# Half of the message sums of a graph network as one-pass products of a rounded part and its rest

## The chip, the cores and the metric

The kernel runs on one core of a Trainium2 chip. A core has a matrix engine (TensorE, PE in the profile; PEld are its weight loads), a vector engine (VectorE, DVE), a scalar engine (ScalarE, ACT), GpSimd (POOL) and a queue for transfers (SyncE, SP). All run at the same time and wait for each other on counters. The metric is device time of the whole program in microseconds (us); lower is better. Before the change three runs gave a median of 3258.17 us (3254.01 to 3269.35).

## The reference

The program is two layers of a graph network with attention, a gated recurrence and experts over 2048 nodes of 512 numbers. The change touches one step, the messages of the second layer:

```
# xn: (2048, 512), edge_attr: (32768, 64), W_e: (64, 512)
msg = jax.nn.relu(x[src] + edge_attr @ W_e + b_e)
aggr = jax.ops.segment_sum(msg, dst, num_segments=x.shape[0])
h = (1.0 + eps) * x + aggr
```

Each of 32768 edges takes the row of its source node, adds its own 64 attributes times a matrix, clips at zero, and is added to the row of its destination node. The inputs `xn_rows` already contain `b_e`. Everything is float32.

## The kernel before

An earlier stage has sorted the edges by destination into buckets of 128 destination rows, padded to whole tiles of 128 edges. A table `sorted_edge` holds for each edge its 64 attributes, the place of its destination within the bucket and its source. Tiles are worked on in pairs: `EG` = 144 pairs, and a pair is of one bucket. For pair `n` these steps run:

- gather (POOL, L2672): two indirect transfers fetch the 2 x 128 source rows into `src`, which has room for four pairs.
- pack (ACT, L2710): once in eight pairs, the attributes are laid side by side in `att`, 64 columns of either tile.
- turn (PE, L2687), eT (ACT, L2716): the 128x128 attributes are transposed into a PSUM bank and copied out as `eT`.
- edge (PE, L2692): two products with `we`, one with the upper and one with the lower 64 rows, into two PSUM banks (banks 2 to 7 serve three pairs in turn).
- raw (DVE, L2738): two additions of 128x512, bank plus `src` into `msg` (three pairs).
- relu (ACT, L2719): clips `msg` in place, 128x1024 in one instruction.
- hot (DVE, L2730): for two pairs at once, the one-hot matrix `hot` of the destinations.
- sum (PE, L2700): two products `hot` by `msg`, accumulated in bank 0 or 1. It sums the messages per destination. Each float32 product is carried out as two instructions.
- add (DVE, L2749): adds the bank to the rows of the bucket in `acc`, at an offset read from a table.

The order on each engine is written by a list: every step of pair `n` has a due time `n + at` (gather -3.6, turn -2.3, eT -2.2, edge -1.75, raw -1.4, relu -0.85, sum 0, add 0.6, hot -2.2), the list is sorted by it, and each engine takes its own steps in that order. An engine's queue is strictly in order: a step that waits holds back all behind it. The waits are those for data (`raw` for the gather and for the edge products, `relu` for `raw`, ...) and those for free buffers (gather `n` for raw `n - 4`, raw `n` for sum `n - 3`, sum `n` for add `n - 2`).

Of the kernel before, what the change touches and what calls it, by code (L numbers as in the profile page):

```python
# [5 lines left out]
F32 = mybir.dt.float32  # L6
I32 = mybir.dt.int32
F32H = mybir.dt.float32r
BF16 = mybir.dt.bfloat16
ALU = mybir.AluOpType  # L10
AF = mybir.ActivationFunctionType
AX = mybir.AxisListType

P = 128
N, D = 2048, 512
# [144 lines left out]
def program(nc, I, const_at, out):  # L160
    PE, ACT, DVE, POOL, SP = nc.tensor, nc.scalar, nc.vector, nc.gpsimd, nc.sync
    everyone = (PE, ACT, DVE, POOL, SP)
    ctx = ExitStack()
    with ctx:
        sig = Signals(nc, ctx)
        pairs = [ctx.enter_context(nc.psum_tensor(f"bank{2 * i}", [P, 2, 512], F32)) for i in range(4)]
        bank = [pairs[i // 2][:, i % 2, :] for i in range(8)]
# [65 lines left out]
        sb = tensors(perf, "perf")  # L233
# [17 lines left out]
        sb = tensors(early, "sort")  # L251
# [23 lines left out]
        hot, run = (va2[:, i * NK * EC:(i + 1) * NK * EC].rearrange("p (b c) -> p b c", b=NK) for i in range(2))  # L275
        src, dst = ends[:, 0, :], ends[:, 1, :]
# [346 lines left out]
        sb = tensors(late, "mix")  # L623
# [392 lines left out]
        PER, SOME = 16, 4  # L1016
# [13 lines left out]
        with ExitStack() as s:  # L1030
            sb = tensors(s, "bias")
            rec = sb("rec", [P, 3, PER, R0])
            hot = sb("hot", [P, 2, PER, P])
# [6 lines left out]
            cleared, rec1_set, apart, prepared, picked, by_pool, by_dve, summed, added = signals = sig.several(9)  # L1040
# [117 lines left out]
        with ExitStack() as s:  # L1158
            sb = tensors(s, "att")
# [313 lines left out]
        with ExitStack() as s:  # L1473
            sb = tensors(s, "route")
# [220 lines left out]
        with ExitStack() as s:  # L1695
            sb = tensors(s, "delta")
# [923 lines left out]
        with ExitStack() as s:  # L2620
            sb = tensors(s, "conv")
            we = sb("we", [P, D])
            HALF = PER // 2
            hot = sb("hot", [P, 2, PER, P])
            src = sb("src", [P, 4, 2, D])
            msg = sb("msg", [P, 3, 2, D])
            eT = sb("eT", [P, 3, P])

            att = sb("att", [P, 2, HALF, P])
            flat = acc[:, :, :].rearrange("p t d -> p (t d)")  # L2630
            we_in = sig.take("hw")
            src_in = sig.several(4, "sw")
            packed, prepared, turned, copied, edge_part, raw, active, summed, added = signals = sig.several(9)


            plan = []
            for n in range(EG):
                for what, at in (("gather", -3.6), ("turn", -2.3), ("eT", -2.2), ("edge", -1.75), ("raw", -1.4), ("relu", -0.85),
                                 ("sum", 0.0), ("add", 0.6)):
                    plan.append((n + at, what, n))  # L2640
                if n % 2 == 0:
                    plan.append((n - 2.2, "hot", n // 2))
                if n % HALF == 0:
                    plan.append((n - 3.0, "pack", n // HALF))
# [19 lines left out]
            def pool():  # L2664
                for _, what, n in plan:
                    if what == "gather":
                        g, k = n // HALF, 2 * (n % HALF)
                        POOL.wait_ge(*rec_in[g % 3].at(16 * (g // 3 + 1)))
                        if n >= 4:
                            POOL.wait_ge(*raw.at(2 * (n - 4) + 2))  # L2670
                        for j in range(2):
                            POOL.indirect_dma_start(  # L2672
                                out=src[:, n % 4, j, :], out_offset=None, in_=xn_rows,
                                in_offset=bass.IndirectOffsetOnAxis(ap=rec[:, g % 3, k + j, 65:66].bitcast(I32), axis=0)
                            ).then_inc(*src_in[n % 4].up(16))

            def tensor():
                PE.wait_ge(*we_in.at(32))
                for _, what, n in plan:
                    if what in ("hot", "pack"):  # L2680
                        continue
                    g, k, q = n // HALF, 2 * (n % HALF), n % 3
                    if what == "turn":
                        PE.wait_ge(*packed.at(g + 1))
                        if n >= 3:
                            PE.wait_ge(*raw.at(2 * (n - 3) + 2))
                        PE.transpose(bank[2 + 2 * q][:, 0:P], att[:, g % 2, k // 2, :], ident).then_inc(*turned.up())  # L2687
                    if what == "edge":
                        PE.wait_ge(*copied.at(n + 1))
                        for j in range(2):  # L2690
                            half = slice(64 * j, 64 * j + 64)
                            a = PE.matmul(bank[2 + 2 * q + j][:, :], eT[half, q, :], we[half, :], start=True, stop=True)  # L2692
                        a.then_inc(*edge_part.up())
                    if what == "sum":
                        PE.wait_ge(*active.at(n + 1))
                        PE.wait_ge(*prepared.at(2 * n // SOME + 1))
                        if n >= 2:
                            PE.wait_ge(*added.at(n - 1))
                        for j in range(2):
                            a = PE.matmul(bank[n % 2][:, :], hot[:, g % 2, k + j, :], msg[:, q, j, :], start=j == 0, stop=j == 1)  # L2700
                        a.then_inc(*summed.up())

            def scalar():
                for _, what, n in plan:
                    q = n % 3
                    if what == "pack":
                        ACT.wait_ge(*rec_in[n % 3].at(16 * (n // 3 + 1)))
                        if n >= 2:
                            ACT.wait_ge(*turned.at((n - 1) * HALF))
                        ACT.activation(att[:, n % 2, :, :].rearrange("p h (j w) -> p (h j) w", j=2), rec[:, n % 3, :, 0:64],  # L2710
                                       AF.Copy).then_inc(*packed.up())
                    if what == "eT":
                        ACT.wait_ge(*turned.at(n + 1))
                        if n >= 3:
                            ACT.wait_ge(*edge_part.at(n - 2))
                        ACT.activation(eT[:, q, :], bank[2 + 2 * q][:, 0:P], AF.Copy).then_inc(*copied.up())  # L2716
                    if what == "relu":
                        ACT.wait_ge(*raw.at(2 * n + 2))
                        ACT.activation(msg[:, q, :, :], msg[:, q, :, :], AF.Relu).then_inc(*active.up())  # L2719

            def vector():
                for _, what, n in plan:
# [9 lines left out]
                    if what == "raw":  # L2732
                        DVE.wait_ge(*edge_part.at(n + 1))
                        DVE.wait_ge(*src_in[n % 4].at(32 * (n // 4 + 1)))
                        if n >= 3:
                            DVE.wait_ge(*summed.at(n - 2))
                        for j in range(2):
                            DVE.tensor_tensor(msg[:, q, j, :], bank[2 + 2 * q + j][:, :], src[:, n % 4, j, :],  # L2738
                                              ALU.add).then_inc(*raw.up())
                    if what == "add":  # L2740
                        if n % 4 == 0:
                            _, starts = nc.values_load_multi_w_load_instructions(
# [507 lines left out]
```

## Time and profile before

| | us |
|---|---|
| median of three timed runs | 3258.17 |
| lowest, highest | 3254.01, 3269.35 |
| span of the profiled execution | 3278.8 |
| messages stage within the span, from the first gather to the last add | 2395.9 to 2842.9 |
| PE busy over the whole span | 2990.0 (91%) |
| POOL busy over the whole span | 1485.6 (45%) |

The profile is of one further execution. Its span counts from the first to the last instruction; no time around it is given on the page, and it is 20.6 us above the median of the timed runs. Busy shares are averages over many stages; what follows concerns the messages stage alone, 437.8 us of steady work at 3.04 us for a pair of tiles (144 pairs).

### The profile page before, as it was taken

How to read it: one execution, taken by the hardware profiler on the slowest of the kernel's cores; microseconds unless marked ns; L12 is line 12 of the kernel's file. 1: busy time of each engine (PE TensorE's matmuls, PEld its weight loads, DVE VectorE, ACT ScalarE, POOL GpSimd, SP SyncE). 2: the span in 40 equal slices, each digit the busy share in tenths (PEclk: the TensorE clock that was granted, in tenths of full speed). 3: DMA queues.
4: the chain of work that ended last, by engine and by line, in shares of the span. 5: the costliest groups of instructions: out<-in, count | busy, mean ns of one | idle time of the engine just before them, and what ended most of it. 6: DMA issues, size and time to landing. Idle time of an engine off the chain costs nothing.

```text
span 3278.8 us, 46022 instructions
## 1 busy us (share of the span) xinstructions
PE 2990.0 (91%) x16081; PEld 1719.2 (52%) x16081; DVE 1674.9 (51%) x3820; ACT 1128.2 (34%) x2501; POOL 1485.6 (45%) x1471
## 2 busy tenths in 40 slices
PE   7999999888999899679999998998999999999828
PEld 3434566577676544357777765444533333444414
DVE  7633266588244432258777632442257777621361
ACT  3312422297122222345666332221034444332201
POOL 0565656498554457333333103554656666300003
PEclk9999999999999899859999778999999999999958
DMA  5400001210111244334554435211167666600404
GB/s 169 138 19 6 13 19 54 68 43 14 42 51 43 69 159 158 125 97 123 135 132 124 123 112 162 83 52 49 30 203 201 205 198 198 160 13 26 175 4 129
DMA packets 275960, 321.36 MB, mean 98 GB/s; under 512 B 155807, under 2 KB 193569, under 8 KB 275732
## 3 DMA queue, kind: packets, MB, share of 16 engines
q1 hardware_dynamic: 219684, 182.57, 18.7%
q0 software_dynamic: 51840, 134.60, 13.6%
q8 instruction: 131, 2.15, 0.3%
q10 hardware_dynamic: 4208, 1.25, 0.2%
q14 instruction: 97, 0.79, 0.1%
HBM read 215.75 MB, written 104.60 MB: 98 GB/s over the span
## 4 chain that ended last, share of the span: by engine, by line
PE 74%; issue 10%; DVE 6%; ACT 4%; POOL 4%; DMA 1%; SPq 0%; ACTq 0%; DVEq 0%; POOLq 0%
PE bank L2700 8%; PE bank L1522 5%; PE bank L2692 5%; PE bank L708 4%; PE bank L1301 3%; PE bank L2363 3%; PE bank L2854 3%; PE bank L2847 3%; PE bank L439 3%; PE bank L731 2%; PE bank L762 2%; PE bank L1117 2%; PE bank L2343 2%; PE bank L1311 2%; PE bank L858 2%
## 5 line engine op out<-in xcount | busy, mean ns | idle before, releaser
L2672 POOL DMA_INDIRECT conv_src<-xn_rows,keep x288 | 272.4, 946 | 176.4 <-DVE conv_msg L2738 111.4
L291 POOL DMA_INDIRECT sorted_bias<-perf_rec,place x256 | 260.2, 1016 | 145.4 <-PE bank L708 90.1
L2700 PE MATMUL bank<-conv_msg,conv_hot 128*128 128x512 f32 x576 | 273.0, 596 | 0.6 <-ACT conv_msg L2719 0.6
L1923 POOL TENSOR_TENSOR delta_dec<-delta_dec,rates_of 128x512 f32<-128x512 f32 x64 | 67.3, 1051 | 338.4 <-ACT delta_dec L1975 338.4
L2738 DVE TENSOR_TENSOR conv_msg<-bank,conv_src 128x512 f32<-128x512 f32 x288 | 185.5, 686 | 47.3 <-PE bank L2692 47.3
L666 POOL DMA_INDIRECT sorted_edge<-rec,place x128 | 127.2, 994 | 141.0 <-PE bank L1362 75.1
L2719 ACT ACTIVATE conv_msg<-conv_msg 128x1024 f32<-128x1024 f32 x144 | 152.0, 1055 | 102.0 <-DVE conv_msg L2738 102.0
L1117 PE MATMUL bank<-bias_prod,bias_hot 128*128 128x256 f32 x640 | 148.2, 387 | 25.2 <-ACT bias_hot L1070 13.1
L2692 PE MATMUL bank<-conv_we,conv_eT 64*128 64x512 f32 x576 | 164.5, 648 | 0.7 <-ACT conv_eT L2716 0.7
L1101 POOL TENSOR_TENSOR bias_prod<-bias_col,bias_rec 128x512 f32<-128x512 f32 x128 | 147.2, 1179 | 16.5 <-PE bank L1117 15.7
L1117 PEld LDWEIGHTS bank<-bias_prod,bias_hot 128*128 128x128 f32 x640 | 120.1, 192 | 53.8 <-issue 28.2
L2164 DVE TENSOR_TENSOR delta_BA<-bank,delta_dec 128x512 f32<-128x512 f32 x128 | 82.2, 683 | 124.3 <-POOL delta_dec L1923 76.7
L2700 PEld LDWEIGHTS bank<-conv_msg,conv_hot 128*128 128x128 f32 x576 | 106.7, 205 | 71.5 <-issue 69.4
L2749 DVE TENSOR_TENSOR acc<-acc,bank 128x512 f32 x144 | 99.0, 688 | 72.7 <-PE bank L2700 72.7
L439 PE MATMUL bank<-xnT,perf_w 128*128 128x512 f32 x256 | 117.0, 600 | 3.6 <-ACT xnT L470 2.1
L3018 POOL TENSOR_TENSOR mlp_mv<-mlp_mv,neg_half 128x1 f32<-128x1 f32 x12 | 6.6, 550 | 242.1 <-DVE mlp_mv L2985 242.1
L2053 PE MATMUL bank<-X 64*128 64x256 f32 x464 | 78.6, 464 | 37.2 <-DVE delta_BA L2164 36.6
L2854 PE MATMUL bank<-mlp_h,keep 128*128 128x512 f32 x256 | 110.5, 592 | 0.0
L2847 PE MATMUL bank<-mlp_hT,mlp_w 128*128 128x512 f32 x256 | 110.4, 592 | 0.0
L889 ACT ACTIVATE mix_ex<-bank,mix_t 128x266 f32<-128x266 f32 x128 | 54.7, 479 | 160.0 <-DVE mix_t L947 160.0
L1079 ACT ACTIVATE bias_far<-C,bias_rec 128x128 f32<-128x128 f32 x320 | 102.2, 390 | 21.1 <-DMA bias_rec<-sorted_bias 14.3
L1932 POOL TENSOR_TENSOR delta_kd<-delta_kv,delta_bg 128x256 f32<-128x256 f32 x64 | 41.4, 646 | 138.2 <-PE bank L2116 138.2
(502 smaller groups left out, 6756.2 us busy)
## 6 DMA issues: line engine op xcount, KB each, us to landing
keep<-slot_qkv SPq DMA_DIRECT2D x32, 512.0 KB, 3.9
delta_kv<-slot_qkv SPq DMA_DIRECT2D x32, 512.0 KB, 3.9
sorted_edge<-sort_pad SPq DMA_DIRECT2D x8, 1440.0 KB, 7.3
keep<-sorted_edge SPq DMA_DIRECT2D x18, 640.0 KB, 5.2
slot_out<-delta_o SPq DMA_DIRECT2D x64, 128.0 KB, 2.0
conv_src<-xn_rows,keep POOLq DMA_INDIRECT x288, 3.6
X<-in_x SPq DMA_DIRECT2D x4, 1024.0 KB, 10.9
sorted_bias<-perf_rec,place POOLq DMA_INDIRECT x256
```

What stands on the lines that cost most here:

```text
L291: POOL.indirect_dma_start(out=sorted_bias, out_offset=bass.IndirectOffsetOnAxis(ap=place[:, 0, c:c + 1], axis=0), in_=rec0[:, c, :], in_of ...
L439: a = PE.matmul(bank[i % 2], w[:, side, c, m * P:(m + 1) * P], xnT[:, c, nb * 512:(nb + 1) * 512], start=c == 0, stop=c == KC - 1)
L1101: engine.tensor_tensor(prod[:, q:q + 2, :, :], col[:, g % 2, k:k + 2, :].unsqueeze(2).broadcast_to([P, 2, H, GW]), rec[:, g % 3, k:k + 2, ...
L1117: a = PE.matmul(bank[u % 8][:, 0:W], hot[:, i // PER % 2, i % PER + j, :], prod[:, i % 8 + j, :, :].rearrange("p h j -> p (h j)"), start=j ...
L1522: a = PE.matmul(bank[3 + n % BANKS], xnT[:, c, t * P:(t + 1) * P], wts[k][:, c, :], start=c == 0, stop=c == KC - 1)
L2672: POOL.indirect_dma_start(out=src[:, n % 4, j, :], out_offset=None, in_=xn_rows, in_offset=bass.IndirectOffsetOnAxis(ap=rec[:, g % 3, k + ...
L2692: a = PE.matmul(bank[2 + 2 * q + j][:, :], eT[half, q, :], we[half, :], start=True, stop=True)
L2700: a = PE.matmul(bank[n % 2][:, :], hot[:, g % 2, k + j, :], msg[:, q, j, :], start=j == 0, stop=j == 1)
L2719: ACT.activation(msg[:, q, :, :], msg[:, q, :, :], AF.Relu).then_inc(*active.up())
L2738: DVE.tensor_tensor(msg[:, q, j, :], bank[2 + 2 * q + j][:, :], src[:, n % 4, j, :], ALU.add).then_inc(*raw.up())
L2847: a = PE.matmul(bank[i % 4], w1[:, c, m * P:(m + 1) * P], hT[:, c, columns(nb)], start=c == 0, stop=c == KC - 1)
L2854: return PE.matmul(bank[4 + nb], w2[:, c, m * P:(m + 1) * P], h1[:, c, columns(nb)], start=c == 0, stop=c == 2 * KC - 1)
```

## The change

`hot` becomes a tile of type `float32r`, a float32 whose value is rounded so that the matrix engine multiplies it in one pass. For every second pair (odd `n`) the clipped messages are split in two: `high` is the message written as `float32r`, and `low` is the message less `high`. Sum `n` is then four one-pass products, `hot` by `high` twice and `hot` by `low` twice. Even pairs keep the float32 products and read `hot` as float32.

- For `n % 4 == 1` ACT clips straight into `high`, and DVE makes `low` with one `scalar_tensor_tensor` (clip, then subtract).
- For `n % 4 == 3` ACT clips twice, into `high` and into `msg`, and POOL makes `low` with one `tensor_tensor` of 128x1024 (in before it has only gathers in this stage).
- raw is one addition of 128x1024 instead of two of 128x512, for all pairs.
- The due times move: gather -3.9, turn -2.7, eT -2.6, edge -2.15, raw -1.8, relu -1.25; new are low at -0.7 (DVE) and -1.0 (POOL).

```
+            hot = sb("hot", [P, 2, PER, P], F32H)
+            high, low = (sb(n, [P, 2, 2, D], F32H) for n in ("high", "low"))
+            def in_halves(n):
+                return n % 2 == 1
-                for what, at in (("gather", -3.6), ("turn", -2.3), ("eT", -2.2), ("edge", -1.75), ("raw", -1.4), ("relu", -0.85),
+                for what, at in (("gather", -3.9), ("turn", -2.7), ("eT", -2.6), ("edge", -2.15), ("raw", -1.8), ("relu", -1.25),
                                  ("sum", 0.0), ("add", 0.6)):
+                if in_halves(n):
+                    plan.append((n - 0.7 if n % 4 == 1 else n - 1.0, "low", n))
...
# POOL
                         if n >= 4:
-                            POOL.wait_ge(*raw.at(2 * (n - 4) + 2))
+                            POOL.wait_ge(*raw.at(n - 3))
...
+                    if what == "low" and n % 4 == 3:
+                        POOL.wait_ge(*active.at(n + 1))
+                        if n >= 4:
+                            POOL.wait_ge(*summed.at(n - 3))
+                        POOL.tensor_tensor(low[:, 1, :, :], msg[:, n % 3, :, :], high[:, 1, :, :].bitcast(F32),
+                                           ALU.subtract).then_inc(*low_by_pool.up())
# PE
+                        if not in_halves(n):
+                            for j in range(2):
+                                a = PE.matmul(bank[n % 2][:, :], hot[:, g % 2, k + j, :].bitcast(F32), msg[:, q, j, :],
+                                              start=j == 0, stop=j == 1)
+                            a.then_inc(*summed.up())
+                            continue
                         for j in range(2):
-                            a = PE.matmul(bank[n % 2][:, :], hot[:, g % 2, k + j, :], msg[:, q, j, :], start=j == 0, stop=j == 1)
+                            PE.matmul(bank[n % 2][:, :], hot[:, g % 2, k + j, :], high[:, n // 2 % 2, j, :], start=j == 0, stop=False)
+                        PE.wait_ge(*(low_by_dve if n % 4 == 1 else low_by_pool).at(n // 4 + 1))
+                        for j in range(2):
+                            a = PE.matmul(bank[n % 2][:, :], hot[:, g % 2, k + j, :], low[:, n // 2 % 2, j, :], start=False,
+                                          stop=j == 1)
                         a.then_inc(*summed.up())
# ACT, in relu
+                        if not in_halves(n):
+                            ACT.activation(msg[:, q, :, :], msg[:, q, :, :], AF.Relu).then_inc(*active.up())
+                            continue
+                        if n >= 4:
+                            ACT.wait_ge(*summed.at(n - 3))
+                        if n % 4 == 1:
+                            ACT.activation(high[:, 0, :, :], msg[:, q, :, :], AF.Relu).then_inc(*active.up())
+                            continue
+                        ACT.activation(high[:, 1, :, :], msg[:, q, :, :], AF.Relu).then_inc(*rounded.up())
+                        ACT.wait_ge(*rounded.at(n // 4 + 1))
                         ACT.activation(msg[:, q, :, :], msg[:, q, :, :], AF.Relu).then_inc(*active.up())
# DVE
-                        for j in range(2):
-                            DVE.tensor_tensor(msg[:, q, j, :], bank[2 + 2 * q + j][:, :], src[:, n % 4, j, :],
-                                              ALU.add).then_inc(*raw.up())
+                        DVE.tensor_tensor(msg[:, q, :, :], pairs[1 + q][:, :, :], src[:, n % 4, :, :], ALU.add).then_inc(*raw.up())
+                    if what == "low" and n % 4 == 1:
+                        DVE.wait_ge(*active.at(n + 1))
+                        if n >= 4:
+                            DVE.wait_ge(*summed.at(n - 3))
+                        DVE.scalar_tensor_tensor(low[:, 0, :, :], msg[:, q, :, :], 0.0, high[:, 0, :, :].bitcast(F32), ALU.max,
+                                                 ALU.subtract).then_inc(*low_by_dve.up())
```

The order on PE, in the middle of the stage, before the change. `conv_att` rows are turn, `conv_eT` rows edge (bank names with numbers; banks 2 to 7 belong to a pair, so turn and edge of one pair have the same bank), `conv_hot` rows sum:

```order
L2687 MATMUL bank4<-C,conv_att 128x128
L2700 MATMUL bank0<-conv_msg,conv_hot 128x512 x2
L2692 MATMUL bank4<-conv_we,conv_eT 128x512 x2
L2687 MATMUL bank6<-C,conv_att 128x128
L2700 MATMUL bank0<-conv_msg,conv_hot 128x512 x2
L2692 MATMUL bank6<-conv_we,conv_eT 128x512 x2
```

The same engine and place after it:

```order
L2719 MATMUL bank0<-conv_high,conv_hot 128x512 x2
L2722 MATMUL bank0<-conv_low,conv_hot 128x512 x2
L2700 MATMUL bank2<-C,conv_att 128x128
L2705 MATMUL bank2<-conv_we,conv_eT 128x512 x2
L2714 MATMUL bank0<-conv_msg,conv_hot 128x512 x2
L2700 MATMUL bank4<-C,conv_att 128x128
L2705 MATMUL bank4<-conv_we,conv_eT 128x512 x2
```

Before, a sum stood between the turn and the edge products of the same pair. Now the edge products follow directly on their own turn.

The order on POOL in the stage after the change (the rows before it were gathers only, 288 in a row; the number at the end counts instructions, so eight gathers are four pairs):

```order
L2679 DMA conv_src<-xn_rows,keep 128x512 x12
L2687 TENSOR_TENSOR conv_low<-conv_msg,conv_high 128x1024
L2679 DMA conv_src<-xn_rows,keep 128x512 x8
L2687 TENSOR_TENSOR conv_low<-conv_msg,conv_high 128x1024
L2679 DMA conv_src<-xn_rows,keep 128x512 x8
```

The first `low` on POOL is that of pair 3 and stands behind the gathers of pairs 0 to 5; the next, of pair 7, stands behind those of pairs 6 to 9. So `low` of pair m stands right before the gathers of pair m+3.

And on DVE, four steps around a `low` of its own (the one of a pair with `n % 4 == 1`), then the addition of the pair two later:

```order
L2770 TENSOR_TENSOR conv_msg<-bank,conv_src 128x1024
L2775 SCALAR_TENSOR_TENSOR conv_low<-conv_msg,conv_high 128x1024
L2779 TENSOR_LOAD bucket
L2786 ISA
L2786 TENSOR_TENSOR acc<-acc,bank 128x512
L2770 TENSOR_TENSOR conv_msg<-bank,conv_src 128x1024
```

The first of these rows is raw of pair n+1, the second low of pair n, the add is that of pair n-1, the last raw of pair n+2, which has `(n+2) % 4 == 3` and whose `low` is POOL's.

## Rows read from the trace of the kernel before

**Rows 1.** The page: the whole execution.
```profile
span 3278.8 us, 46022 instructions
```

**Rows 2.** Windows, mid-stage: PE, PEld, DVE, ACT, POOL busy us; PE clock, DMA share, GB/s.
```profile
2600.00:2650.00 50.00, 50.00 (x151) 17.25 (x148) 37.52 (x59) 23.30 (x36) 31.32 (x34) 1.00 0.69 200
```

**Rows 3.** Timeline mid-stage: start us, duration us, engine, line, operation, out<-in.
```profile
2600.67 1.29 DVE L2738 TENSOR_TENSOR conv_msg<-bank,conv_src 128x512 f32<-128x512 f32 x2 [0.28 <-PE bank L2692]
...
2602.53 1.13 PE L2692 MATMUL bank<-conv_we,conv_eT 64*128 64x512 f32 x4
...
2603.59 0.33 PE L2687 MATMUL bank<-C,conv_att 128*128 128x128 f32 x1
...
2603.76 1.88 PE L2700 MATMUL bank<-conv_msg,conv_hot 128*128 128x512 f32 x4
...
2605.57 1.13 PE L2692 MATMUL bank<-conv_we,conv_eT 64*128 64x512 f32 x4
```

**Rows 4.** Groups by line, the stage: busy us, mean ns, idle before, releaser.
```profile
L2672 POOL DMA_INDIRECT conv_src<-xn_rows,keep x288 | 272.4, 946 | 176.4 <-DVE conv_msg L2738 111.4 <-issue 65.0
...
L2719 ACT ACTIVATE conv_msg<-conv_msg 128x1024 f32<-128x1024 f32 x144 | 152.0, 1055 | 102.0 <-DVE conv_msg L2738 102.0
...
L2749 DVE TENSOR_TENSOR acc<-acc,bank 128x512 f32 x144 | 99.0, 688 | 72.7 <-PE bank L2700 72.7
```

**Rows 5.** Timeline elsewhere: one-pass products of float32r, one after the other.
```profile
1599.83 0.58 PE L2043 MATMUL bank<-delta_dec_half,delta_after_half 128*128 128x512 f32 x1
...
1600.02 0.19 PEld L2044 LDWEIGHTS bank<-delta_dec_half,delta_after_half 128*128 128x128 f32 x1
...
1600.24 0.40 PE L2044 MATMUL bank<-delta_dec_half,delta_after_half 128*128 128x512 f32 x1
```

**Rows 6.** Timeline, the stage's start: turn, eT and edge of pair 1; two gathers.
```profile
2400.94 0.95 POOL L2672 DMA_INDIRECT conv_src<-xn_rows,keep  x1 [0.30 <-issue]
...
2401.45 0.47 PE L2687 MATMUL bank<-C,conv_att 128*128 128x128 f32 x1
...
2401.96 0.28 ACT L2716 ACTIVATE conv_eT<-bank 128x128 f32<-128x128 f32 x1 [2.57 <-PE bank L2687]
2402.19 0.95 POOL L2672 DMA_INDIRECT conv_src<-xn_rows,keep  x1 [0.30 <-issue]
...
2402.29 1.22 PE L2692 MATMUL bank<-conv_we,conv_eT 64*128 64x512 f32 x2 [0.37 <-ACT conv_eT L2716]
```

**Rows 7.** Groups by shape: POOL operations on two tiles, three forms.
```profile
L1923 POOL TENSOR_TENSOR delta_dec<-delta_dec,rates_of 128x512 f32<-128x512 f32 x64 | 67.3, 1051 | 338.4 <-ACT delta_dec L1975 338.4
...
L2528 POOL TENSOR_TENSOR X<-X,lin_bo 128x512 f32<-128x512 f32 x16 | 20.3, 1269 | 3.5 <-DMA lin_rec<-in_edge_attr 3.2
...
L317 POOL TENSOR_TENSOR perf_rec<-perf_rec,sort_be 128x1664 f32<-128x1664 f32 x1 | 3.7, 3672 | 0.0
```

**Rows 8.** Timeline of POOL: an indirect transfer behind an operation.
```profile
1190.06 2.93 POOL L1581 TENSOR_TENSOR route_ss<-route_ss,neg_half 128x16 f32<-128x16 f32 x1
1193.18 1.02 POOL L1569 DMA_INDIRECT slot_qkv<-route_rw,slot_of  x1 [0.20 <-issue]
```

**Rows 9.** Line L2139 of DVE, 128x1024: count, duration ns min/median/max.
```profile
L2139 DVE SCALAR_TENSOR_TENSOR delta_Us<-delta_Bs,delta_strict x8: 1218/1225/1226, 1400.9 to 1854.7; 128x1024 f32<-128x1024 f32 x8
```

**Rows 10.** Line L2672, the gathers of the stage: time to landing.
```profile
DMA to landing us min/median/max: 3.2/3.6/7.7
```

**Rows 11.** Timeline of POOL: an earlier gather, for whose landing DVE waited.
```profile
2015.25 0.97 POOL L2289 DMA_INDIRECT merge_ab<-slot_out,slot_of  x1 [0.31 <-issue]
```

**Rows 12.** Line L2289 at that gather alone: its time to landing.
```profile
DMA to landing us min/median/max: 6.9/6.9/6.9
```

**Rows 13.** Timeline of DVE: the instruction that waited for it.
```profile
2022.22 0.49 DVE L2425 TENSOR_SCALAR merge_ab<-merge_ab,slot_w 128x512 f32<-128x512 f32 x1 [6.09 <-DMA merge_ab<-slot_out,slot_of]
```

**Rows 14.** Windows of a stage in which PE pauses briefly (columns as in rows 2).
```profile
2092.00:2118.00 26.00, 24.63 (x81) 12.47 (x81) 11.63 (x25) 5.62 (x10) 15.17 (x13) 1.00 0.27 81
```

**Rows 15.** Windows of a stage in which PE pauses for longer.
```profile
1100.00:1130.00 30.00, 21.62 (x122) 14.52 (x121) 15.61 (x33) 5.59 (x10) 18.24 (x19) 0.77 0.31 109
```

More of the change, by code:

```diff
@@ L2623, in program @@
             HALF = PER // 2
-            hot = sb("hot", [P, 2, PER, P])
+            hot = sb("hot", [P, 2, PER, P], F32H)
             src = sb("src", [P, 4, 2, D])
             msg = sb("msg", [P, 3, 2, D])
+            high, low = (sb(n, [P, 2, 2, D], F32H) for n in ("high", "low"))
             eT = sb("eT", [P, 3, P])
@@ L2632, in program @@
             src_in = sig.several(4, "sw")
-            packed, prepared, turned, copied, edge_part, raw, active, summed, added = signals = sig.several(9)
+            (packed, prepared, turned, copied, edge_part, raw, active, rounded, low_by_dve, low_by_pool,
+             summed, added) = signals = sig.several(12)
+            def in_halves(n):
+                return n % 2 == 1
             plan = []
             for n in range(EG):
-                for what, at in (("gather", -3.6), ("turn", -2.3), ("eT", -2.2), ("edge", -1.75), ("raw", -1.4), ("relu", -0.85),
+                for what, at in (("gather", -3.9), ("turn", -2.7), ("eT", -2.6), ("edge", -2.15), ("raw", -1.8), ("relu", -1.25),
                                  ("sum", 0.0), ("add", 0.6)):
                     plan.append((n + at, what, n))
+                if in_halves(n):
+                    plan.append((n - 0.7 if n % 4 == 1 else n - 1.0, "low", n))
                 if n % 2 == 0:
@@ L2685, in tensor @@
                         if n >= 3:
-                            PE.wait_ge(*raw.at(2 * (n - 3) + 2))
+                            PE.wait_ge(*raw.at(n - 2))
                         PE.transpose(bank[2 + 2 * q][:, 0:P], att[:, g % 2, k // 2, :], ident).then_inc(*turned.up())
@@ L2717, in scalar @@
                     if what == "relu":
-                        ACT.wait_ge(*raw.at(2 * n + 2))
+                        ACT.wait_ge(*raw.at(n + 1))
+                        if not in_halves(n):
[8 more added lines that the diff above has]
+                        ACT.wait_ge(*rounded.at(n // 4 + 1))
                         ACT.activation(msg[:, q, :, :], msg[:, q, :, :], AF.Relu).then_inc(*active.up())
```

## Prediction

> **What bounds the kernel now.** I read the span first [rows 1], then the windows of the messages stage, to see which engine has no idle time there. PE is busy for all 50 of 50 us at a granted clock of 1.00 (its upper level, 2.4 GHz), DVE for 37.5, ACT for 23.3, POOL for 31.3 [rows 2]. The timeline then gives PE's period: edge at 2602.53, turn at 2603.59, sum at 2603.76, the next edge at 2605.57 [rows 3]. So edge takes 1.06, turn 0.17, sum 1.81, together 3.04 us for a pair and 12.16 us for four pairs, without a gap. PE sets the stage, 144 pairs by 3.04 = 437.8 us.
>
> The groups by line show what lies beside it [rows 4]. DVE, ACT and POOL all wait for PE directly or by one step. POOL needs a second look, since the change gives it work. Its 288 gathers take 946 ns each, 272 us. But they are not all of it: where POOL waits for nothing, gathers start 1.25 us apart (2400.94, 2402.19), with 0.30 us of "issue" in between [rows 6]. Eight gathers (four pairs) so need 10.0 of 12.16 us. POOL is 82% occupied, not 62%.
>
> **The change part by part.** I count in groups of four pairs, of which there are 36.
>
> *Removed on PE.* A sum of an odd pair is four one-pass products instead of two full ones. Such products stand elsewhere in the trace: two in a row end at 1600.41 and 1600.64, 0.23 us apart, and the second's weight load (0.19) fits beside the first [rows 5]. Four take 0.92, against 1.81: 0.89 us less, 72 times, 64 us less if nothing else moved. Bounds: none below 0.23; at most as the full product, 0.45 each.
>
> *Moved on PE.* The new due times put the edge products directly behind the turn of their own pair. They need eT, which needs the turn, so PE now waits through ACT's copy. The stage's start shows exactly this order: turn at 2401.45 (0.47), eT at 2401.96 (0.28), edge at 2402.29 [rows 6]. The links are 0.04 and 0.05. With the turn's 0.33 us at full clock [rows 3], from turn to edge takes 0.33 + 0.04 + 0.28 + 0.05 = 0.70 us, where it took 0.17: 0.53 us more in each of 144 pairs, 76 us. By PE alone four pairs then take 4 x (0.70 + 1.06) + 2 x 1.81 + 2 x 0.92 = 12.50 us. This is already 0.34 more than now, 12 us for the stage.
>
> *Added on POOL.* Once in four pairs a subtraction of 128x1024. The width isn't in the trace. For two whole tiles POOL took 1.269 us at 512 and 3.672 at 1664 columns; a straight line gives 2.086 ns a column and 2.34 us at 1024 [rows 7]. Upper bound twice 1.269 = 2.54. Lower bound about 1.9: the 1.051 of an operation whose second tile is a broadcast [rows 7], carried by the same line's fixed part of 0.20. I take 2.34, since both operands here are whole. The next gather starts 0.20 us behind it [rows 8]. POOL alone needs 9.9 + 2.34 = 12.24 us for four pairs, no less than PE's old period: POOL can't give anything back either.
>
> *Added on DVE.* raw is one instruction of 1024 instead of two; low for `n % 4 == 1` is one of 1024. A two-operand instruction of that width takes 1.22 us [rows 9]. Two raws back to back took 1.29 [rows 3]; at 0.69 for one of this width, as the add has [rows 4], the second starts 0.08 before the first ends, so I count 1.14 and 0.61 for the occupation by 1024 and 512. Four raws, a low, four adds and two hots (as an add) make 4.6 + 1.1 + 2.4 + 1.2 = 9.3 of the period: hidden as a load, but not as an order, see below.
>
> *Added on ACT.* One relu in four is done twice, 1.055 us more [rows 4]; 36 x 1.06 = 38 us of an engine that is half idle. Hidden as a load too.
>
> *The wait that is added.* In POOL's order the low of pair m (m % 4 = 3) stands right before the gathers of pair m+3. It needs relu m, which needs raw m, which needs gather m, and behind it are queued the gathers that feed the next such chain. I follow it around, from the start of low m to that of low m+4:
>
> - low m 2.34 + 0.20, then the first gather of pair m+3: 2.54
> - its second gather starts 1.25 later and lands 3.6 us after its start [rows 6, 10]: 7.39. (That landing counts from the start is seen at an earlier gather: 2015.25 + 6.9 = 2022.15, and the instruction that waited for it starts at 2022.22 [rows 11 to 13].)
> - raw m+3 starts 0.04 later, 7.43, and holds DVE 1.14: 8.57
> - in DVE's order now come its own low (pair m+2), 1.14, and the add of pair m+1, 0.61: 10.32. Raw m+4, whose gathers landed at 9.89, starts only here.
> - raw m+4 takes 1.22 + 0.04: 11.58
> - relu twice, the second waiting for the first, 2 x (1.055 + 0.04): 13.77. Low m+4 starts.
>
> Of these the gathers of pairs m+3 to m+6 need only 12.24, so POOL stands idle 1.5 us before each low; PE's own 12.50 fits as well. The period is 13.77 us: 13.77 - 12.16 = 1.61, times 36 = 58 us. PE is then paced by the gathers instead of the other way around, and its 64 us are gone twice over.
>
> With the ends of the unknowns: low at 1.9 and landing at the least of 3.2 give 12.93, +28 us. Low at 2.54 and landing at 4.0 (rec loads share the queues) give 14.37, +80. At the stage's two ends the pipeline fills once either way; I count nothing.
>
> Two pages of the Trainium skill bear on this. "GPSIMD Engine Reference", Engine selection, advises VectorE for elementwise work on a tile, since GpSimd is about twice as slow with two inputs; the table of Elementwise gives 4497 ns at 2048 columns. The trace agrees (1.269 against 0.688 at 512 [rows 4, 7]). By half of the page's figure as an estimate, 2.25, the period would be 13.68 and the sum 55 us.
>
> **The rivals.**
>
> *A, the long way round does not bind, but PE or POOL alone does.* If relu m is done earlier than I follow it, the bound is PE's 12.50: +12 us, 3270. For it: the gathers' buffers are four deep and POOL has nothing else. Against it: every link above has a row. This is under the 0.5% (16 us) that a measurement of this kernel can tell from no change.
>
> *B, the other side: PE keeps its bound and gains what was meant.* Mechanism: eT is ready when PE reaches the edge products, and POOL fits its low between gathers. Then four pairs take 12.16 - 1.78 = 10.38 us, -64 us, 3194. For any gain at all POOL's eight gathers and its low must fit in 12.16, so low must stay under 2.26 us, and from turn to edge must take under 0.61; for the whole gain it must take 0.17, and POOL must need 10.38. The rows speak against each.
>
> *C, PE's clock falls in the new pauses.* PE will be idle nearly a quarter of the stage. In a stage with short pauses (1.4 of 26 us) the clock stayed at 1.00 [rows 14]; in one with 8.4 of 30 idle, in longer pieces, its mean was 0.77 [rows 15]. No pause I count here is over 0.9 us. If the mean fell to 0.77, PE would need about 12.50 / 0.77 = 16.2 us: +146 us, 3404.
>
> *D, DVE and POOL hold each other up.* Their lows would overlap, and one would wait for the other's 1.22 us: 15.0, +102, 3360. In my walk POOL's low runs from 0 to 2.34 and DVE's from 8.57 to 9.71, so they don't meet. "SBUF — State Buffer", Who interferes with whom, says that a DVE instruction with two SBUF inputs contends with a GpSimd one that reads SBUF; by that rule low and hot on DVE qualify, raw and add (one input in PSUM) don't. No row here isolates it.
>
> *E, the change doesn't do what it says:* the products stay at 0.45 us. PE alone then needs 14.3 us, +76. Rows 5 speak against it.
>
> **How the numbers follow.** The sum is made in the profiled execution: 3278.8 + 58 = 3337 us of span. That span is 20.6 us over the median of the timed runs, but the stage repeats at 3.04 us throughout, so I put the same 58 on the median: 3258.2 + 58 = 3316 us. Chances: the chain as followed, between +28 and +80, 0.74; A 0.12; B 0.03; C 0.03; D 0.04; E 0.04. The range of the likeliest alone is 3286 to 3338. To hold 8 in 10 I widen it to 3280 to 3342, which takes in most of E. Slower by over 0.5% hold the chain, C, D, E and a little of A: 0.87. Within 0.5%: the rest of A, 0.09. Faster: B and an error of the whole walk, 0.04.
>
> **What the profile will show.** The stage about 500 us long; PE at some 75 to 80% in it; four products of an odd pair 0.23 us apart; about 0.37 us of PE waiting for eT before most edge products; POOL's low at 2.3 to 2.4 us, with some 1.5 us of waiting for ACT before each (55 us in all), and gathers 1.25 us apart behind it; raws waiting for landings of src, not for edge products. I am wrong if POOL waits for raw rather than for relu, if low is far from 2.34, or if PE has no gaps.

## The result, and the profile after

| | before | after |
|---|---|---|
| median of timed runs, us | 3260.31 (3254.01 to 3269.35, 4 runs) | 3330.74 (3327.39 to 3350.51, 4 runs) |
| ratio, 95% interval | 1 | 1.0224 [1.0188, 1.0259] |
| span of the profiled execution, us | 3278.8 | 3329.5 |
| messages stage, first turn to last add, us | 444.3 (2398.6 to 2842.9) | 520.4 (2371.4 to 2891.8) |

The change made the kernel 2.2% slower. 3316 was forecast, with a range of 3280 to 3342. The stage alone grew by 76.1 us. The two spans differ by only 50.7, because the profiled execution of before came to the stage 27.2 us later (2398.6 against 2371.4). The code ahead of the stage is the same in all kernels here, and their profiled executions enter the stage anywhere from 2371 to 2409. The two differ in PE's clock on the way: up to 2365 us it stood at its lower level for 256 us in before and for 188 in after. So where one execution is compared with another, the length of the stage says more than the span.

The page's span, which answers to [rows 1]:

```profile
span 3329.5 us, 46133 instructions
```

And three windows of the stage, in the columns of [rows 2]:

```profile
2450.00:2500.00 50.00, 41.48 (x134) 16.17 (x134) 34.40 (x40) 24.32 (x35) 39.08 (x34) 1.00 0.58 176
2600.00:2650.00 50.00, 43.49 (x131) 16.59 (x132) 34.59 (x40) 23.94 (x34) 35.73 (x31) 0.94 0.52 162
2700.00:2750.00 50.00, 41.53 (x132) 15.72 (x129) 34.11 (x41) 25.43 (x35) 38.08 (x32) 1.00 0.54 168
```

Before, PE was busy for 50 of 50 us. Now it is for 41.5 at full clock, and no other engine is full either: POOL has 39, DVE 34. When no engine is full and the time has still grown, a chain of waits sets the pace. POOL's low shows where it closes (duration least, median, most in ns; then who was waited for, us and times):

```profile
L2687 POOL TENSOR_TENSOR conv_low<-conv_msg,conv_high x36: 2342/2358/2372, 2389.1 to 2887.4; 128x1024 fp32r<-128x1024 f32 x36
its engine sat idle before it (us, times) until:
  ACT conv_msg L2752: 55.6, 36
```

It takes 2.36 us where 2.34 was interpolated from [rows 7], and POOL idles 55.6 us for relu before it where 55 was forecast. One turn of the loop in the timeline of POOL, DVE and ACT (start, duration, engine, line; other rows left out):

```profile
2716.04 2.35 POOL L2687 TENSOR_TENSOR conv_low<-conv_msg,conv_high 128x1024 fp32r<-128x1024 f32 x1 [0.24 <-ACT conv_msg L2752]
...
2718.54 0.95 POOL L2679 DMA_INDIRECT conv_src<-xn_rows,keep  x1
...
2719.80 0.95 POOL L2679 DMA_INDIRECT conv_src<-xn_rows,keep  x1 [0.30 <-issue]
...
2723.54 1.22 DVE L2770 TENSOR_TENSOR conv_msg<-bank,conv_src 128x1024 f32<-128x1024 f32 x1 [2.19 <-issue]
...
2724.68 1.22 DVE L2775 SCALAR_TENSOR_TENSOR conv_low<-conv_msg,conv_high 128x1024 fp32r<-128x1024 f32 x1
...
2724.97 1.74 POOL L2679 DMA_INDIRECT conv_src<-xn_rows,keep  x1 [0.30 <-issue]
...
2725.81 0.68 DVE L2786 TENSOR_TENSOR acc<-acc,bank 128x512 f32 x1
...
2726.41 1.22 DVE L2770 TENSOR_TENSOR conv_msg<-bank,conv_src 128x1024 f32<-128x1024 f32 x1
...
2727.66 1.06 ACT L2750 ACTIVATE conv_high<-conv_msg 128x1024 fp32r<-128x1024 f32 x1 [0.56 <-DVE conv_msg L2770]
...
2728.75 1.06 ACT L2752 ACTIVATE conv_msg<-conv_msg 128x1024 f32<-128x1024 f32 x1
...
2729.89 2.36 POOL L2687 TENSOR_TENSOR conv_low<-conv_msg,conv_high 128x1024 fp32r<-128x1024 f32 x1 [0.24 <-ACT conv_msg L2752]
```

These are the six steps of the forecast, in their order. Over all 35 intervals between lows on POOL:

| link | forecast, us | measured, us |
|---|---|---|
| low m to the second gather of pair m+3 | 3.79 | 3.76 |
| that gather to raw m+3 (landing) | 3.64 | 4.04 mean (3.40 to 6.75) |
| raw m+3, DVE's low, add, to raw m+4 | 2.89 | 2.95 mean (2.87 in most, up to 3.54) |
| raw m+4 to the clip into high | 1.26 | 1.26 mean (1.25 to 1.40) |
| to the clip into msg | 1.10 | 1.09 |
| to low m+4 | 1.10 | 1.14 |
| the whole | 13.77 | 14.24 mean (13.56 to 16.85) |

The landing varies in every turn. In 5 of the 35 turns raw m+4 also waits, by 0.2 to 0.6 us: in four it starts 0.08 us after the landing of its own gathers, in one it waits for its edge products, at a granted clock of 0.50. The other links are nearly the same throughout. PE's new order, in the timeline of PE and ACT, beside [rows 3, 6]:

```profile
2722.84 0.27 PE L2700 MATMUL bank<-C,conv_att 128*128 128x128 f32 x1
2723.15 0.28 ACT L2739 ACTIVATE conv_eT<-bank 128x128 f32<-128x128 f32 x1 [1.91 <-PE bank L2700]
...
2723.48 1.13 PE L2705 MATMUL bank<-conv_we,conv_eT 64*128 64x512 f32 x4 [0.37 <-ACT conv_eT L2739]
```

From turn to edge it takes 0.64 us, with 0.37 of waiting (0.70 and 0.37 were forecast; the turn, measured alone, is 0.27 and not 0.33).

The groups of the stage from 2380 to 2880, as in [rows 4]:

```profile
L2679 POOL DMA_INDIRECT conv_src<-xn_rows,keep x279 | 290.0, 1039 | 79.5 <-issue 72.1 <-DVE conv_msg L2770 3.0
L2770 DVE TENSOR_TENSOR conv_msg<-bank,conv_src 128x1024 f32<-128x1024 f32 x140 | 171.2, 1223 | 143.3 <-issue 102.4 <-PE bank L2705 31.7 <-DMA conv_src<-xn_rows,keep 9.1
L2705 PE MATMUL bank<-conv_we,conv_eT 64*128 64x512 f32 x562 | 163.4, 658 | 52.2 <-ACT conv_eT L2739 52.2
```

Two readings differ from the forecast. A gather's mean went from 946 to 1039 ns. And the idle time before raw is mostly put down to "issue", only 9.1 us to a landing, though it was forecast as waiting for landings. In the turn above, the edge product for the raw at 2723.54 stood at 2719.96 and was over by 2721.09, so it was not what was waited for. The gather at 2719.80, asked for by itself, shows what was:

```profile
DMA to landing us min/median/max: 3.7/3.7/3.7
```

It landed at 2723.5, and the raw starts at 2723.54. Set side by side, raw m+3 starts 0.08 us after the landing of its second gather in 33 of the 35 turns. So the landing ends this wait, though the profile puts it down to "issue".

### The profile page after: what moved, and what is told of

Its sections match the earlier page's. It is cut to its first block, busy times and chain, and to the rows that moved or that the text cites. A ratio compares the mean times of both kernels' runs of the same rounds, so it can differ in the third digit from the quotient of the medians.

```text
span 3329.5 us, 46133 instructions
## 1 busy us (share of the span) xinstructions
PE 2947.6 (89%) x16081; PEld 1709.2 (51%) x16081; DVE 1692.1 (51%) x3712; ACT 1163.1 (35%) x2537; POOL 1596.7 (48%) x1507
## 3 DMA queue, kind: packets, MB, share of 16 engines
q8 instruction: 131, 2.15, 0.3%
q10 hardware_dynamic: 4208, 1.25, 0.2%
## 4 chain that ended last, share of the span: by engine, by line
PE 60%; issue 16%; POOL 11%; DVE 7%; ACT 4%; DMA 3%; SPq 0%; ACTq 0%; POOLq 0%; DVEq 0%
POOL conv_src L2679 7%; PE bank L1522 5%; PE bank L708 4%; PE bank L1301 3%; PE bank L2363 3%; PE bank L2891 3%; PE bank L2884 3%; PE bank L439 3%; PE bank L1117 3%; PE bank L731 2%; PE bank L762 2%; PE bank L2343 2%; PE bank L858 2%; PE bank L1311 2%; POOL delta_dec L1923 2%
## 5 line engine op out<-in xcount | busy, mean ns | idle before, releaser
L2679 POOL DMA_INDIRECT conv_src<-xn_rows,keep x288 | 298.6, 1037 | 96.8 <-issue 89.4
L2770 DVE TENSOR_TENSOR conv_msg<-bank,conv_src 128x1024 f32<-128x1024 f32 x144 | 176.1, 1223 | 152.9 <-issue 104.9
L2714 PE MATMUL bank<-conv_msg,conv_hot 128*128 128x512 f32 x288 | 150.9, 648 | 0.0
L2687 POOL TENSOR_TENSOR conv_low<-conv_msg,conv_high 128x1024 fp32r<-128x1024 f32 x36 | 84.8, 2357 | 55.6 <-ACT conv_msg L2752 55.6
L2739 ACT ACTIVATE conv_eT<-bank 128x128 f32<-128x128 f32 x144 | 39.9, 277 | 190.4 <-PE bank L2700 190.2
L2705 PEld LDWEIGHTS bank<-conv_we,conv_eT 64*128 64x128 f32 x576 | 44.8, 190 | 117.2 <-ACT conv_eT L2739 117.2
```

The lines of the kernel that those rows point to most:

```text
L2679: POOL.indirect_dma_start(out=src[:, n % 4, j, :], out_offset=None, in_=xn_rows, in_offset=bass.IndirectOffsetOnAxis(ap=rec[:, g % 3, k + ...
L2714: a = PE.matmul(bank[n % 2][:, :], hot[:, g % 2, k + j, :].bitcast(F32), msg[:, q, j, :], start=j == 0, stop=j == 1)
L2770: DVE.tensor_tensor(msg[:, q, :, :], pairs[1 + q][:, :, :], src[:, n % 4, :, :], ALU.add).then_inc(*raw.up())
```

## The experiments

The theory (T): the loop over POOL sets the pace, and PE's new order costs 12 us beneath it. The rivals: PE's order alone (A), the clock (C), DVE and POOL holding each other up (D). Runs of one group ran on one chip beside the kernel before.

| run | what | ratio to before, 95% | time less before, us | stage, us |
|---|---|---|---|---|
| x1 | before, new due times only | 1.0209 [1.0177, 1.0240] | +69 | 511.6 |
| x2 | after, all lows on DVE | 1.0036 [1.0011, 1.0061] | +12 | 456.9 |
| x3 | after, turn early | 1.0256 [1.0216, 1.0295] | +82 | 516.4 |
| x4 | x2 and x3 | 0.9979 [0.9955, 1.0004] | -7 | 437.5 |
| x5 | after, POOL's low 0.15 later | 1.0125 [1.0069, 1.0180] | +40 | 477.9 |
| x6 | x5 and x3 | 1.0081 [1.0048, 1.0115] | +24 | 474.5 |
| x7 | x4, raw kept in PSUM | 0.9877 [0.9823, 0.9931] | -30 | 394.1 |
| y1 | before, one more addition on DVE | one run | +2 | 444.2 |
| y2 | before, one more reduction on DVE | one run | +2 | 443.9 |

x1 to x4 stood beside a before of 3260.72 us, x5, x7, y1 and y2 beside one of 3254.20. Beside x6 the kernel before took 3304.80, so for x6 only the ratio can be compared with the rest. y1 and y2 ran once each.

### x1: the order alone

```
# before.py
-  ("gather", -3.6), ("turn", -2.3), ("eT", -2.2), ("edge", -1.75), ("raw", -1.4), ("relu", -0.85)
+  ("gather", -3.9), ("turn", -2.7), ("eT", -2.6), ("edge", -2.15), ("raw", -1.8), ("relu", -1.25)
```

> The kernel before with nothing but the six new due times (gather -3.9, turn -2.7, eT -2.6, edge -2.15, raw -1.8, relu -1.25): no split, nothing added on POOL, DVE or ACT. Theory 1 (two costs side by side: the new order on PE, turn directly before its own edge products, and the loop through POOL's low): the order alone costs 0.53 us in each pair, 4 x (0.70 + 1.06 + 1.81) = 14.3 us for four pairs against 12.16, so +76 us on before, with a PE wait for eT of about 0.37 us in each pair. Rival 2 (only the split and its extra work cost time, the order is free because PE has slack elsewhere): within 10 us of before.

Measured: 3329.97 us, +69. The timeline of its PE alone:

```profile
2599.85 0.27 PE L2687 MATMUL bank<-C,conv_att 128*128 128x128 f32 x1
2600.49 1.13 PE L2692 MATMUL bank<-conv_we,conv_eT 64*128 64x512 f32 x4 [0.37 <-ACT conv_eT L2716]
2601.55 1.98 PE L2700 MATMUL bank<-conv_msg,conv_hot 128*128 128x512 f32 x4
2603.37 0.27 PE L2687 MATMUL bank<-C,conv_att 128*128 128x128 f32 x1
```

The period is 3.52 us (turn to turn) against 3.04, and (3.52 - 3.04) x 144 = 69. So six numbers in a list cost as much as the whole change, with every product as before. The term of +76 was 7 too large, mostly by the turn's 0.27 instead of 0.33.

### x2: no work on POOL

```
# after.py
-  plan.append((n - 0.7 if n % 4 == 1 else n - 1.0, "low", n))
+  plan.append((n - 0.7, "low", n))
-  POOL.tensor_tensor(low[:, 1, :, :], msg[:, n % 3, :, :], high[:, 1, :, :].bitcast(F32), ALU.subtract)
+  # every odd pair clips once, into high; DVE makes low for all of them
```

> The changed kernel with every low made on DVE from one clipped copy (for n % 4 == 3 ACT clips once, into high, and DVE clips and subtracts, as for n % 4 == 1); POOL has gathers only; due time of low -0.7 for all. Theory 1: the loop through POOL is gone, and PE's own order is what is left, 12.50 us for four pairs: +12 us on before, 50 to 60 us less than the changed kernel. Rival 2 (DVE's load or its wider instructions hold the stage): DVE gets 1.14 us more in four pairs, so the time stays at +70 or rises. Rival 3 (the one-pass products are slower than 0.23 us in this stage): it stays above +40.

Measured: 3272.34, +12. Four pairs take 12.51 us in the middle of the stage, and 12.50 was forecast for PE's own need. That this fits so well is partly luck, as two errors cancel: each turn was taken 0.06 us too long (0.24 in four pairs), and four one-pass products were taken 0.12 too short (1.04 us here and not 0.92, 0.24 in two sums). The loop thus costs the rest, some 58 us of 70, and A is what remains without it. PE now waits only for eT (51.7 us in the stage).

### x3: the turn early, the loop left in

```
# after.py
-  ("turn", -2.7), ("eT", -2.6) ... plan.append((n - 3.0, "pack", n // HALF))
+  ("turn", -3.1), ("eT", -3.05) ... plan.append((n - 3.4, "pack", n // HALF))
```

> The changed kernel with turn at -3.1, eT at -3.05 and pack at -3.4, so that sum n-3 stands between turn n and edge n on PE again; low stays on POOL. Theory 1: PE's own need falls to 10.4 us for four pairs, but the loop POOL low, gathers, landing, raw, low, add, raw, clip, clip stays at 13.8 or more: +60 to +70 us on before, no different from the changed kernel by more than 10 us, with more idle time on PE. Rival 2 (the waits for eT on PE set the stage): down by 50 us or more.

Measured: 3343.06, +82, outside the upper end of what was expected. The mechanism is the one expected: taking PE's waits for eT away gains nothing, and the mean interval between POOL's lows is 14.18 us (14.24 in after). The 12 us by which the whole is above after don't lie in the stage, which is even 4 us shorter (516.4 against 520.4). In the profiled executions, 10.1 us apart, x3 entered the stage 13.5 us later (2384.9 against 2371.4), with the same code ahead of it. The granted clock in the stage from 2450 to 2800 was 0.94 against 0.98, and the stage is no longer for it.

### x4: both, a miss

> Both edits together: low on DVE alone, turn before the sum again. Theory 1: neither cost is left, PE's 10.4 us for four pairs (or DVE's 10.4, which is as much) sets the stage: 10.4 to 11.0 us, 40 to 60 us less than before, so 3200 to 3220. If one of the two edits alone were the whole cause, this run would be no better than that one.

Measured: 3253.81, -7, where -40 to -60 was expected. Here PE (326.5 of 350 us) and DVE (311.2) were nearly full, and so, unseen in its busy time of 275.9, was POOL. DVE and POOL in its timeline, and its gathers as a group:

```profile
2602.21 1.21 DVE L2764 SCALAR_TENSOR_TENSOR conv_low<-conv_msg,conv_high 128x1024 fp32r<-128x1024 f32 x1
2602.28 1.96 POOL L2679 DMA_INDIRECT conv_src<-xn_rows,keep  x1 [0.30 <-issue]
```

```profile
L2679 POOL DMA_INDIRECT conv_src<-xn_rows,keep x280 | 328.6, 1174 | 88.3 <-issue 81.2 <-DVE conv_msg L2759 7.1
```

A gather issued beside DVE's low takes 1.96 us instead of 0.95. With a mean of 1.174 and 0.31 between them, eight gathers need 11.9 us for four pairs. In the middle of the stage four pairs take 11.94 (12.15 in before). So POOL by itself fills the period, and nearly all idle time before a gather is "issue". x7 tests this below. This gave the next question: which DVE instructions do it?

### y1 and y2: the disputed cost by itself

```
# before.py, on DVE at the relu of every odd pair; "more" holds fixed numbers and feeds nothing
+  y1: DVE.tensor_tensor(more[:, 2, :], more[:, 0, :], more[:, 1, :], ALU.add)         # reads two SBUF tiles
+  y2: DVE.tensor_reduce(more[:, 2, 0:8], more[:, 0, :] in eight parts, AX.X, ALU.add) # reads one
```

> The kernel before with one more DVE instruction in every second pair: an addition of two fixed SBUF tiles, 128x1024, 1.22 us, that waits for nothing and feeds nothing. Theory 4: gathers that run beside it are stretched by up to its length; the mean goes from 946 to about 1050 ns or more, single ones near 2 us. Rival 5: 946 as before. PE's period of 12.16 us for four pairs should hold or rise by a little (POOL 10.0 + 2 x about 1).

> The same with a reduction of one fixed SBUF tile, 128x1024 to 128x8, also 1.22 us, at the same place in DVE's order. Theory 4: it has one SBUF operand, so gathers stay at 946 ns in the mean and none is stretched to 2 us. If any long DVE instruction did it, this run would look as the one with two operands.

Measured: both near before in time (3256.45 and 3256.26), since PE still binds. But the gathers differ. From y1, its timeline, then its group:

```profile
2602.79 1.22 DVE L2744 TENSOR_TENSOR conv_more<-conv_more 128x1024 f32<-128x1024 f32 x1
...
2603.02 1.80 POOL L2673 DMA_INDIRECT conv_src<-xn_rows,keep  x1 [0.35 <-issue]
```

```profile
L2673 POOL DMA_INDIRECT conv_src<-xn_rows,keep x282 | 322.9, 1145 | 104.6 <-issue 103.4 <-DVE conv_msg L2741 1.1
```

From y2, the same two views:

```profile
2602.15 1.22 DVE L2744 TENSOR_REDUCE conv_more<-conv_more 128x8 f32<-128x1024 f32 x1
...
2602.39 0.94 POOL L2673 DMA_INDIRECT conv_src<-xn_rows,keep  x1 [0.36 <-issue]
```

```profile
L2673 POOL DMA_INDIRECT conv_src<-xn_rows,keep x281 | 266.2, 947 | 159.4 <-DVE conv_msg L2741 85.7 <-issue 73.7
```

Both DVE instructions last 1.22 us and a gather starts about 0.23 us into either. Beside two SBUF inputs it takes 1.80, beside one 0.94. The reduction also writes less (8 columns against 1024), but x7 below has a DVE instruction that writes 1024 with one SBUF input and holds no gather. So D exists, but between DVE and a gather. DVE's low and POOL's never overlapped in after, so what the two would do to each other isn't shown.

### x5: the loop opened by one number

```
# after.py: POOL's low behind the next pair's gathers, not before them
-  plan.append((n - 0.7 if n % 4 == 1 else n - 1.0, "low", n))
+  plan.append((n - 0.7 if n % 4 == 1 else n - 0.85, "low", n))
```

> The changed kernel with one number changed: POOL's low is due at -0.85 instead of -1.0, so that it stands behind the gathers of pair m+3 instead of before them. Theory 1: the loop from low m to low m+4 then holds only the gathers of pair m+4: 2.54 + 1.25 + 3.64 + 1.26 + 2 x 1.10 = 10.9 us and no longer binds; POOL's load (12.24) and PE's order (12.50) do, so +12 to +20 us on before, some 50 us less than the changed kernel, and POOL's wait for ACT before low (55.6 us there) nearly gone. Rival 2 (POOL's load with low on it is the bound, wherever low stands): no change.

Measured: +40 (3294.37), against +70 of after. By the ratios it is 1.0224 - 1.0125 = 0.0099, 32 us; the stage is 42.5 us shorter. The loop was the cause: no instruction is another, only one stands elsewhere, and POOL's wait for relu falls from 55.6 to 9.9 us. But +12 to +20 was expected. The group of the lows and of the gathers of x5, and its DVE and POOL at one place:

```profile
L2679 POOL DMA_INDIRECT conv_src<-xn_rows,keep x279 | 291.8, 1046 | 79.9 <-issue 69.4 <-DVE conv_msg L2770 10.1 <-PE bank L2722 0.3
L2687 POOL TENSOR_TENSOR conv_low<-conv_msg,conv_high 128x1024 fp32r<-128x1024 f32 x36 | 85.6, 2379 | 10.5 <-ACT conv_msg L2752 9.9
```

```profile
2604.47 1.22 DVE L2775 SCALAR_TENSOR_TENSOR conv_low<-conv_msg,conv_high 128x1024 fp32r<-128x1024 f32 x1
...
2604.81 1.69 POOL L2679 DMA_INDIRECT conv_src<-xn_rows,keep  x1 [0.30 <-DVE conv_msg L2770]
```

POOL now hardly rests: 8 x 1.046 + 7 x 0.30 + 0.16 + 2.38 = 13.01 us, and lows are 13.03 us apart. POOL's own 12.24 had left the stretched gathers out.

### x6: the loop opened and the turn early

The edits of x5 and x3 together.

> Low on POOL at the later place (-0.85) and turn before the sum again. With the later place alone the period was 13.03 us, POOL never idle: eight gathers 9.9, low 2.38, and 0.74 by which one gather was stretched beside DVE's low. Theory 4 (POOL's load with the stretching is what was left there): PE's order now costs nothing but changes nothing either, the period stays at 12.9 to 13.2, and the time at +30 to +45 us on before. Rival 2 (PE's waits for eT held that version, POOL only just kept up): the period falls to 12.3 or less, +5 us or less on before.

Measured: 1.0081, by 3258 some +26 (+24 beside its own before); lows 12.95 us apart, within the 12.9 to 13.2 expected. The time missed the expected +30 to +45 from below. Its stage is 3.4 us shorter than x5's. POOL is the bound, and an earlier turn moves little.

### x7: no DVE instruction of 1024 with two SBUF inputs

```
# x4's kernel: raw stays in its PSUM banks; relu and DVE's low read it there
-  DVE.tensor_tensor(msg[:, q, :, :], pairs[1 + q][:, :, :], src[:, n % 4, :, :], ALU.add)
+  DVE.tensor_tensor(pairs[1 + q][:, :, :], pairs[1 + q][:, :, :], src[:, n % 4, :, :], ALU.add)
-  DVE.scalar_tensor_tensor(low[...], msg[:, q, :, :], 0.0, high[...], ALU.max, ALU.subtract)
+  DVE.scalar_tensor_tensor(low[...], pairs[1 + q][:, :, :], 0.0, high[...], ALU.max, ALU.subtract)
...
+  # turn n waits for low or relu of pair n - 3 instead of its raw; relu waits for sum n - 3, raw no longer does
```

> The version with low on DVE and turn before the sum (+0 on before so far, gathers of 1.17 us in the mean against 0.95), with raw written back into its PSUM banks and clip and low reading it there. DVE's low then has one operand in SBUF instead of two. Theory 4 (a DVE instruction with two SBUF operands stretches the gather that runs beside it, to 1.96 us beside low and 1.38 beside hot, and POOL so became the bound at about 11.8 us for four pairs): gathers beside low are 0.95 again, mean under 1.05, POOL needs 10.4, and the stage falls to 10.6 to 11.2 us for four pairs, 30 to 50 us less than before. Rival 5 (DVE's own load or PE's clock held that version): gathers may shorten, the time does not move by 10 us. Risk: the banks are held longer, some 7 us of the 7.8 there are.

Measured: 3224.52 against 3254.20, ratio 0.9877: 30 us faster by the medians, 40 by the ratio, and faster than both kernels. The stage is 50.2 us shorter than in before. Its windows, then DVE and POOL at the place that answers to that of x4:

```profile
2450.00:2800.00 350.00, 343.60 (x1185) 139.94 (x1186) 336.33 (x385) 179.99 (x271) 246.56 (x244) 1.00 0.75 216
```

```profile
2603.22 1.21 DVE L2766 SCALAR_TENSOR_TENSOR conv_low<-bank,conv_high 128x1024 fp32r<-128x1024 f32 x1
2603.29 0.95 POOL L2679 DMA_INDIRECT conv_src<-xn_rows,keep  x1 [0.30 <-issue]
```

The gather beside low takes 0.95 again (1.96 in x4), and the mean of all is 1007 ns, which with 0.31 between them makes 10.5 us for eight. Four pairs take about 10.6 us, near rival B's 10.38, the whole gain meant. It took three things: no low on POOL, the turn early, and the gathers left alone. PE and DVE are both nearly full; the stage ends at 2788.4, and from 2450 to 2780 they are busy for 327.3 and 325.7 of 330 us. The edit also freed raw from its wait for a sum and gave ACT another source, which no run takes apart. In x4 hardly any idle time before a raw was put down to a sum (of 41 us from 2420 to 2800, 23 to "issue" and 17 to the edge products), so the first of these is an unlikely cause.

## Why the prediction was right, and what it missed

- **The loop binds: right.** The six links came in the order written, and five had their size to 0.06 us. x5 opens the loop with one number and gets 32 us back; x2 removes it and leaves +12.
- **Its size: the landing was mis-sized.** 3.64 us was taken from a median [rows 10]; in the loop it was 4.04 in the mean, just past my upper end of 4.0. That is 0.40 of the 0.47 us by which the period was too short; 0.06 more came mostly from the few turns in which raw m+4 had a wait of its own. 0.47 times 36 is 17 us: 58 + 17 = 75, against the 76 by which the stage grew. Landings did not grow (over all 288 the mean is 3.98 in after). Their times are skewed, and a loop that waits for one in every turn pays the mean and not the median. The trace of before had it: its 288 gathers land after a median of 3.6 us and a mean of 4.03. With that mean the same walk gives 14.20 us, +73. In the loop's own 35 landings the median is 3.66 and the mean 3.94, before the 0.08 us to the start of raw, where 0.04 was counted.
- **PE's order: right in mechanism, 0.06 too much a pair.** x1 alone gives +69 for the +76. In after it is hidden beneath the loop: PE needs 12.5 of 14.24 us. Rival A is what x2 shows, at +12 by two errors that cancel.
- **The one-pass products: right, but sized too short.** Inside a sum they stand 0.23 us apart as in [rows 5]. The step from the first to the second and the last one's step to the product behind it are in part longer (up to 0.34), so four take more than the 0.92 counted: 1.04 us in x2. From edge product to edge product an odd pair takes 2.25 us in x7 and an even one 3.04, 0.79 less and not 0.89. Rival E falls. The 64 us are 57 (0.79 times 72), and only x7 gets at them.
- **POOL's low: right**, 2.36 for 2.34. "GPSIMD Engine Reference" of the Trainium skill, Elementwise, would have given 2.25 by half its figure: 0.1 low.
- **Rival C, the clock: present, but small.** Between 2596.9 and 2599.9 PE waited 1.37, 0.17 and 0.37 us; from 2600 to 2606 the granted clock was 0.50, the lower level of 1.2 GHz, and the four instructions of a sum took 3.78 us for 1.98. The stage's mean from 2450 to 2800 was 0.98. A pause of 1.37 is more than the 0.9 that I had counted: there PE waited for DVE's low, a wait that the forecast doesn't have and that makes 30.3 us from 2380 to 2880.
- **Rival D: asked in the wrong form.** I let only low meet low, found that they don't, and stopped. What meets low and hot on DVE are the gathers. In after it cost little, as POOL has 1.5 us of slack a turn (at most the 0.06 us above, where a gather of pair m+4 was held); in x4, x5 and x6 it was the bound. My sum for POOL, 12.24, was wrong for that reason, without harm to the forecast.
- **PE's busy share** is 83% at full clock, where 75 to 80% was forecast. I had taken the waits off the period; the profile counts a product until its modelled end, which may be the difference. It is not settled, and no term rests on it.

## What to carry to other kernels

When a strictly ordered queue gets a step that needs results, follow what stands behind it around to itself: the period of that loop can be longer than any engine's work, and moving the step past one neighbour may open it. Where such a loop waits for a transfer in every turn, count the mean of its landing times and not the median. Before moving a producer right next to its consumer, count the trip over the other engine once for every time it is made. And where a queue issues gathers, see which vector instructions with two SBUF inputs run when one is issued, since those hold it.

## What the hardware showed that was not expected

A gather is held by a DVE instruction with two SBUF inputs, in a sharp way. From 2425 to 2800 us I set each gather against the low or hot (or the added addition) that it overlapped, in after, x4, x7, y1 and y2. In 263 cases it was stretched. In every one of them it had started while the DVE instruction was already running (0.04 to 1.07 us into it), and its end came 0.81 to 0.83 us after DVE's, whatever its start. Alone a gather takes 0.95. So, as an estimate from these two, it is held from about 0.13 us after its own start until DVE ends: in x4 DVE ends at 2603.42, the gather at 2604.24. A gather that started before the DVE instruction, or in its first 0.03 us, was not stretched. Nor was any of the 70 that overlapped x7's low, which reads one operand from PSUM, nor any of 65 by y2's reduction (two of these were held by hot, which ran before it). The Trainium skill, "SBUF — State Buffer", Who interferes with whom, has the rule for the cause: a DVE instruction with two SBUF inputs contends with a GpSimd one that reads SBUF. The runs agree. The same section infers that such an addition doesn't hold the making of a transfer's descriptors; for these indirect transfers, which read their row numbers from SBUF, y1 shows that it does, 1145 against 947 ns in the mean.
